# The last feed-forward of a four-layer block: its two-part products in reduced float32 become single products in plain float32

## The reference, cut to what matters

```python
def ternary_quant(w):
    s = jnp.mean(jnp.abs(w))
    q = jnp.clip(jnp.round(w / s), -1.0, 1.0) * s
    return w + jax.lax.stop_gradient(q - w)
w1q = ternary_quant(w1)
w3q = ternary_quant(w3)
w2q = ternary_quant(w2)
h1 = jnp.einsum('bsd,hd->bsh', x, w1q)
h3 = jnp.einsum('bsd,hd->bsh', x, w3q)
g = jax.nn.silu(h1) * h3
return jnp.einsum('bsh,dh->bsd', g, w2q)
...
x = x + jnp.tanh(g_ffn[3]) * _L3_ffn_ref(_layernorm(x, axis=-1), L3_ffn_w1, L3_ffn_w3, L3_ffn_w2)
```

## Time and profile before

| | us |
|---|---|
| median of 3 executions | 2648.24 |
| fastest, slowest | 2644.77, 2649.71 |
| the profiled execution, its own time | 2647.07 |
| its span, first to last instruction | 2645.3 |
| mean granted TensorE clock | 0.947 |
| TensorE matmul busy | 2398.7 (91%) |
| TensorE weight loads busy | 1413.4 (53%) |
| VectorE, ScalarE, GpSimd busy | 992.7, 656.1, 463.8 |

### The profile page before, as it was taken

The page is one execution under the profiler, slowest core; times in us unless marked ns, Lnnn a source line. Parts: engine busy times, 40 slices in busy tenths (PEclk is TensorE's granted clock), DMA queues, the critical chain, the costliest instruction groups (busy, mean ns, idle before and its releaser), DMA issues. The chain is left out here.

```text
span 2645.3 us, 34842 instructions
## 1 busy us (share of the span) xinstructions
PE 2398.7 (91%) x10421; PEld 1413.4 (53%) x10422; DVE 992.7 (38%) x2413; ACT 656.1 (25%) x1456; POOL 463.8 (18%) x616
## 2 busy tenths in 40 slices
PE   7898999988888899998989999695999999789898
PEld 4344444453664566666546654253656665345476
DVE  5534353534334333334412224651222221612375
ACT  2344443530110433433101110110111111051221
POOL 6000000003122100000321114234111111700061
PEclk9999999988999899999889999777999999989999
DMA  9101010013774000000436664150544452561220
GB/s 371 68 1 33 0 33 0 0 33 112 254 227 126 28 17 5 13 13 23 139 102 203 197 194 118 48 160 25 162 131 152 157 170 71 155 211 43 83 84 28
DMA packets 151926, 263.88 MB, mean 100 GB/s; under 512 B 16406, under 2 KB 80510, under 8 KB 151325
## 3 DMA queue, kind: packets, MB, share of 16 engines
q1 hardware_dynamic: 117789, 186.08, 21.8%
q0 software_dynamic: 19072, 49.35, 6.5%
q10 hardware_dynamic: 14976, 27.27, 2.7%
HBM read 212.77 MB, written 49.88 MB: 99 GB/s over the span
## 5 line engine op out<-in xcount | busy, mean ns | idle before, releaser
L360 POOL DMA_INDIRECT slot_list<-token_ids,slots x64 | 62.0, 969 | 620.2 <-DVEq L546 601.3
L924 PE MATMUL bank<-f2r_wd,f2b_hT 128*128 (+1 forms) x300 | 137.2, 593 | 1.4 <-DVE f2b_hT L1028 1.4
L250 PE MATMUL bank<-ident,xn 112*128 112x112 f32 x256 | 59.3, 399 | 86.5 <-DVE xn L226 86.5
L905 PE MATMUL bank<-f2r_wg,f2b_xT 128*128 x400 | 128.9, 466 | 1.6 <-ACT f2b_xT L961 1.3
L905 PE MATMUL bank<-f2r_wu,f2b_xT 128*128 x400 | 126.5, 459 | 0.0
L1355 PE MATMUL bank<-l0a_vo,l0a_zT 128*112 128x512 f32 x256 | 115.5, 594 | 2.9 <-DVE l0a_zT L1513 2.9
L1325 PE MATMUL bank<-l_kvcT,xnT 128*112 128x375 f32 x256 | 98.4, 508 | 20.7 <-DVE l0a_qrT L1485 20.7
L1416 ACT ACTIVATE l0a_p<-l0a_p,l0a_low 112x375 f32<-112x375 f32 x128 | 77.1, 607 | 115.2 <-DVE l0a_low L1506 114.0
L1015 DVE TENSOR_TENSOR f2b_h<-bank,f2b_acted 128x352 f32<-128x352 f32 x50 | 26.2, 525 | 205.9 <-PE bank L905 205.9
L360 POOL DMA_INDIRECT slot_list<-token_ids,slots_in x32 | 31.2, 974 | 408.5 <-DVEq L546 399.3
L1496 DVE CUSTOM_DVE_ANT_0 l0a_p<-bank,xn 112x375 f32<-112x375 f32 x128 | 70.3, 549 | 83.5 <-PE bank L1327 83.3
(11 more groups left out here) (374 smaller groups left out, 4470.0 us busy)
## 6 DMA issues: line engine op xcount, KB each, us to landing
slot_rows<-zeros SPq DMA_DIRECT2D x2, 7424.0 KB
slot_rows<-f2b_y ACTq DMA_DIRECT2D x50, 256.0 KB, 3.7
f1r_wg<-in_l_wg SPq DMA_DIRECT2D x16, 704.0 KB, 4.6
f1r_wu<-in_l_wu SPq DMA_DIRECT2D x16, 704.0 KB, 6.4
f2r_wg<-in_l_wg SPq DMA_DIRECT2D x16, 704.0 KB, 4.4
f2r_wu<-in_l_wu SPq DMA_DIRECT2D x16, 704.0 KB, 6.2
xn<-in_l_w_ffn SPq DMA_DIRECT2D x11, 768.0 KB, 4.2
l_raw<-in_l_w_ffn SPq DMA_DIRECT2D x11, 768.0 KB, 4.2
```

The lines of the kernel that those rows point to most:

```text
L250: mm = pe.transpose(s.bank[n % 4][:, k * TOK:(k + 1) * TOK], s.xn[:, n, k * 128:(k + 1) * 128], s.ident[0:TOK, 0:TOK])
L360: pool.indirect_dma_start(s.slot_list, bass.IndirectOffsetOnAxis(ap=slots[:, k, b:b + 1], axis=0), s.token_ids[:, b:b + 1], None, **bound) ...
L905: mm = pe.matmul(bank[:, 0:width], xT[:, v, k, :], w[:, bass.ds(at, 1), k, :].rearrange("p o f -> p (o f)"), start=(k == 0), stop=(k == KD ...
L924: mm = pe.matmul(bank_y[v][:, :], hT[0:fn, v, c, :], wd[0:fn, bass.ds(at, 1), c, :].rearrange("p o f -> p (o f)"), start=(c == 0), stop=(c ...
```

## The change

The ternary tiles, and the hidden values, become plain float32 tiles, the activations are no longer split, and the parts, their remainders, the tile `h` and the semaphores between them go. `piece(n)` makes 8 calls where it made 16, each on `s.xnT` itself, `output(u)` half as many as well. `hidden(n)` writes straight into `hT` (now one part), and so takes over the wait of L2286 for the output of unit u - 2; output waits for `h_done`. The order of pieces, outputs, ternary tiles and additions stays, and so do the loads.

```diff
--- before.py
+++ after.py
@@ -2197,15 +2197,12 @@
         def sb(n, shape, dt=F32):
             return ctx.enter_context(nc.sbuf_tensor(f"f3_{n}", shape, dt))
 
-        below_done, tern_done, xhi_done, xlo_done, g_done, u_done, act_done, h_done, hi_done, lo_done, y_done, y_added = s.sems(
-            "f3", "below_done", "tern_done", "xhi_done", "xlo_done", "g_done", "u_done", "act_done", "h_done", "hi_done",
-            "lo_done", "y_done", "y_added")
+        below_done, tern_done, g_done, u_done, act_done, h_done, y_done, y_added = s.sems(
+            "f3", "below_done", "tern_done", "g_done", "u_done", "act_done", "h_done", "y_done", "y_added")
         below = sb("below", [128, 2, D])
-        tern = sb("tern", [128, TERNS, 3, D], F32R)
-        xr = sb("xr", [128, 2, KD, NT], F32R)
+        tern = sb("tern", [128, TERNS, 3, D])
         acted = sb("acted", [128, 2, HALF])
-        h = sb("h", [128, 2, HALF])
-        hT = sb("hT", [128, 2, 2, UNIT, NT], F32R)
+        hT = sb("hT", [128, 2, UNIT, NT])
         block = ctx.enter_context(nc.Block())
 
         def halves(half):
@@ -2237,29 +2234,22 @@
                 if n >= 2:
                     pe.wait_ge(h_done, n - 1)
                 for m, done in ((0, g_done), (1, u_done)):
-                    for part in range(2):
-                        if n < 2 and m == 0:
-                            pe.wait_ge((xhi_done, xlo_done)[part], half + 1)
-                        for k in range(KD):
-                            mm = pe.matmul(s.bank[2 * (n % 2) + m][:, 0:HALF],
-                                           tern[:, c % TERNS, m, k * 128:(k + 1) * 128],
-                                           xr[:, part, k, halves(half)],
-                                           start=(part == 0 and k == 0), stop=(part == 1 and k == KD - 1))
+                    for k in range(KD):
+                        mm = pe.matmul(s.bank[2 * (n % 2) + m][:, 0:HALF],
+                                       tern[:, c % TERNS, m, k * 128:(k + 1) * 128],
+                                       s.xnT[:, k, halves(half)], start=(k == 0), stop=(k == KD - 1))
                     mm.then_inc(done, 1)
 
             def output(u):
                 chunks = [c for c in range(L3_CHUNKS) if unit_of[c] == u]
                 pe.wait_ge(tern_done, 3 * chunks[-1] + 3)
-                pe.wait_ge(lo_done, 2 * chunks[-1] + 2)
+                pe.wait_ge(h_done, 2 * chunks[-1] + 2)
                 for b in range(B):
                     if u * B + b >= 4:
                         pe.wait_ge(y_added, u * B + b - 3)
                     for c in chunks:
-                        for part in range(2):
-                            mm = pe.matmul(s.bank[4 + b % 4][0:TOK, :],
-                                           hT[:, u % 2, part, c % UNIT, b * TOK:(b + 1) * TOK],
-                                           tern[:, c % TERNS, 2, :],
-                                           start=(c == chunks[0] and part == 0), stop=(c == chunks[-1] and part == 1))
+                        mm = pe.matmul(s.bank[4 + b % 4][0:TOK, :], hT[:, u % 2, c % UNIT, b * TOK:(b + 1) * TOK],
+                                       tern[:, c % TERNS, 2, :], start=(c == chunks[0]), stop=(c == chunks[-1]))
                     mm.then_inc(y_done, 1)
 
             for n in range(PIECES):
@@ -2270,23 +2260,12 @@
 
         @block.scalar
         def _(act):
-            for half in range(2):
-                act.activation(xr[:, 0, :, halves(half)], s.xnT[:, :, halves(half)], ACT.Copy).then_inc(xhi_done, 1)
-            for n in range(PIECES + 1):
-                if n < PIECES:
-                    act.wait_ge(g_done, n + 1)
-                    if n >= 2:
-                        act.wait_ge(h_done, n - 1)
-                    act.activation(acted[:, n % 2, :], s.bank[2 * (n % 2)][:, 0:HALF], ACT.Silu,
-                                   scale=t.scale[:, 0:1]).then_inc(act_done, 1)
-                if n >= 1:
-                    c, half = (n - 1) // 2, (n - 1) % 2
-                    u = unit_of[c]
-                    act.wait_ge(h_done, n)
-                    if u >= 2:
-                        act.wait_ge(y_done, (u - 1) * B)
-                    act.activation(hT[:, u % 2, 0, c % UNIT, halves(half)], h[:, (n - 1) % 2, :], ACT.Copy)\
-                       .then_inc(hi_done, 1)
+            for n in range(PIECES):
+                act.wait_ge(g_done, n + 1)
+                if n >= 2:
+                    act.wait_ge(h_done, n - 1)
+                act.activation(acted[:, n % 2, :], s.bank[2 * (n % 2)][:, 0:HALF], ACT.Silu,
+                               scale=t.scale[:, 0:1]).then_inc(act_done, 1)
 
         @block.vector
         def _(dve):
@@ -2300,27 +2279,16 @@
                                              scalar=t.half[:, m:m + 1], in1=below[:, i % 2, :],
                                              op0=ALU.is_gt, op1=ALU.subtract).then_inc(tern_done, 1)
 
-            def rest_of_xnT(half):
-                dve.wait_ge(xhi_done, half + 1)
-                dve.tensor_tensor(xr[:, 1, :, halves(half)], s.xnT[:, :, halves(half)],
-                                  xr[:, 0, :, halves(half)].bitcast(F32), ALU.subtract).then_inc(xlo_done, 1)
-
             def hidden(n):
+                c, half = n // 2, n % 2
+                u = unit_of[c]
                 dve.wait_ge(u_done, n + 1)
                 dve.wait_ge(act_done, n + 1)
-                if n >= 2:
-                    dve.wait_ge(hi_done, n - 1)
-                    dve.wait_ge(lo_done, n - 1)
-                dve.scalar_tensor_tensor(out=h[:, n % 2, :], in0=s.bank[2 * (n % 2) + 1][:, 0:HALF],
+                if u >= 2:
+                    dve.wait_ge(y_done, (u - 1) * B)
+                dve.scalar_tensor_tensor(out=hT[:, u % 2, c % UNIT, halves(half)], in0=s.bank[2 * (n % 2) + 1][:, 0:HALF],
                                          scalar=t.scale[:, 1:2], in1=acted[:, n % 2, :],
                                          op0=ALU.mult, op1=ALU.mult).then_inc(h_done, 1)
-
-            def rest_of_hidden(n):
-                c, half = n // 2, n % 2
-                u = unit_of[c]
-                dve.wait_ge(hi_done, n + 1)
-                dve.tensor_tensor(hT[:, u % 2, 1, c % UNIT, halves(half)], h[:, n % 2, :],
-                                  hT[:, u % 2, 0, c % UNIT, halves(half)].bitcast(F32), ALU.subtract).then_inc(lo_done, 1)
 
             def add(u):
                 for b in range(B):
@@ -2331,19 +2299,13 @@
                                              scalar=t.output_scale[0:TOK, :], in1=s.x[:, b, :],
                                              op0=ALU.mult, op1=ALU.add).then_inc(y_added, 1)
 
-            make_ternary(0, (0, 1))
-            rest_of_xnT(0)
-            rest_of_xnT(1)
-            make_ternary(0, (2,))
+            make_ternary(0, range(3))
             for n in range(PIECES):
                 if n % 2 == 0 and n // 2 + 1 < L3_CHUNKS:
                     make_ternary(n // 2 + 1, range(3))
                 hidden(n)
-                if n:
-                    rest_of_hidden(n - 1)
                 if n > 1 and n % (2 * UNIT) == 1:
                     add(unit_of[n // 2] - 1)
-            rest_of_hidden(PIECES - 1)
             add(units - 1)
```

## The result

| | before | after |
|---|---|---|
| median, us | 2647.41 (4 runs) | 2740.77 (4 runs) |
| fastest, slowest | 2644.77, 2649.71 | 2738.04, 2742.50 |
| profiled execution, its own time | 2647.07 | 2739.71 |
| its span | 2645.3 | 2738.0 |
| TensorE in the stage, first gate/up record to the end of the last output record | 119.8 | 211.5 |

The changed kernel takes 1.0353 times as long, with a 95% interval of 1.0337 to 1.0369: 93 us more. The kernel before has one execution more here than it had at the time of the prediction, 2646.59 us, which moves its median from 2648.24 to 2647.41.

What follows compares the result with a forecast made beforehand. TensorE was taken as the bound: gate/up 132.4, output 75.5, start 2.2, last seam 0.8 and modelled ends 0.3 make 211.2 us against 119.8. That adds 91.4 to 2648.24, giving 2739.6 us, range 2735 to 2744.5.

Steps and rivals of the forecast that it cites:

- The price of a record: TensorE's last feed-forward: 352 gate/up records at 0.376 us make 132.4 us, 176 output records at 0.429 make 75.5.
- The start: First gate/up pieces: TensorE starts at 2516.46 again, and 4.5 us at half clock lose 2.2 us.
- modelled end: Last records before the last seam and of the stream: shown ends lie past the start distance, 0.3 us together.
- The last seam: Before the last output: TensorE waits for `hidden` alone, 0.8 us in place of 2.09.
- The stretch: TensorE's whole stream in the last feed-forward: 211.2 us against 119.8.
- Cover: Last feed-forward: nothing on VectorE or GpSimd is waited for after 2520; TensorE alone is late.
- Splitting: Remainders on VectorE, 16.3 us for the hidden values, cost only the first pieces' wait and the seams.
- same records at the same price: Rival for TensorE's stream: record count matters, not type; 115.9 us, 3.9 less, 2644.3; chance 0.01.
- The rule on weight loads: TensorE's full-height loads: hidden beside the matmul by the trace, against the skill page; the sum counts none.
- The rival of loads in the open: Each TensorE weight load stands between matmuls: 305.4 us in place of 207.9, time 2837; chance 0.005.
- One record per call: Rival: float32 calls leave one record at today's price, TensorE needs 56.3 us, GpSimd sets the end, 2590.8; chance 0.01.

Runs made afterwards that it cites:

- The run with the clock kept up: Changed kernel with six more float32 matmuls of 448 columns ahead of the first piece; stretch 209.0 us, 1.0315 times the kernel before.
- the run on the fourth chip: The changed kernel itself, measured again on another chip against the kernel before there; stretch 211.1 us, ratio 1.0342.
- the doubled kernel: Changed kernel with float32r operands, each call made twice on the same rounded part, remainders left out; stretch 115.1 us, 0.9987 times the kernel before.
- the kernel cut to 224 columns: Kernel before with each gate/up call cut into two of 224 moving columns; stretch 124.8 us, one run of 2693.5 us beside a median of 2692.2.
- The one-part kernel: Changed kernel with float32r operands, one call each on the rounded part, remainders left out; stretch 77.6 us, 0.9836 times the kernel before.

## Why the prediction was right, point by point

The median is 2740.77 for a forecast of 2739.6; the profiled execution took 2739.71 for 2738.5, its span 2738.0 for 2736.7. The rise is 93.4 us by the medians and 92.6 by the profiled executions, for 91.4.

- **The price of a record.** 36.08 / 96 = 0.376 and 20.60 / 48 = 0.429 us, as read from L2026, L2033 and L741. The counts stayed. These two terms are 207.9 of the 211.5 us.
- **The start.** TensorE waited for the same two tiles. The clock rose 4.7 us after the first record where I took 4.5; the first 128 records cost 50.71 - 128 x 0.376 = 2.6 us too much, of which 0.16 are the modelled end that the sum counts apart, so 2.4 where the sum has 2.2. The run with the clock kept up shows that this is the clock's. That it came so close is in part luck: in the run on the fourth chip the clock rose 4.0 us after the first record, and in the one with float32 in gate/up only 5.1, behind the same idle stretch.
- **The last seam.** 0.82 us for 0.8.
- **The stretch.** 211.5 for 211.2.
- **The rest of the 1.3 us of span.** The stage's loads begin 0.7 us later (2500.40 for 2499.71), ahead of anything changed, and the first record 0.2 later behind that.
- **Cover.** No wait for `f_below` or `f_tern` reached TensorE after the first. The waits of VectorE for TensorE grew instead: the additions waited 52.8 us.
- **Splitting.** It was put at nothing but stall and seams; the doubled kernel gives it 4.7 us of stretch. The forecast's own way of counting it (same records at the same price) gave 3.9; most of the rest is the 0.234 us of an output record, read too high by the modelled end that it holds (0.230 in a stream without seams).
- **The rule on weight loads.** The Trainium skill, page "TensorE: Matmul & The Clock Gate", section "The mechanism" (the prediction named the section behind it), lets a load overlap matmuls in flight only in another row group. The trace disagrees more plainly than the prediction had it: a full-height load takes 112 ns of a stream of 8 columns, and with 224 columns, 93 ns at 2.4 GHz, the records still stand 112 ns apart (the kernel cut to 224 columns). One after the other they would take 205.
- **What was right for too weak a reason.** I argued that today's loads of 192 ns fit a distance of 203 ns. That reads as though loads were nearly the bound of a float32r call. They are not, since a load takes 112 ns of the stream; my expectation for the 224 columns rested on it and missed by some 60 us. The rival of loads in the open was priced by the shown durations, 190 and 174 ns (the second is the median of L2259's loads in the trace and stands in no row shown); at 112 ns for each of the 528 it would have come at most 59 us later than the forecast, not 97.5.
- **A rival that was too low.** "One record per call" was put at 2590.8 by GpSimd's busy time. The one-part kernel shows such a stage: 42 us less than before, not 57, since VectorE's row of tiles, hidden values and additions is the longer one and TensorE's clock fell in the waits.

## What to carry to other kernels

Count the records that a call leaves before counting calls: a plain float32 product leaves two, each two cycles per column, so it costs 3.7 float32r products, and two float32r products on a split operand are the cheaper way as long as the split hides elsewhere. Two are enough here because the weights are -1, 0 and 1 and need no second part; a product of two general operands would need more, and no run here prices that. Splitting that looks like much work (16 us on VectorE) was worth under 5 us here, since TensorE was the bound; the idle engines' busy time is no saving. The same shapes elsewhere in a kernel, read from start to start in a stretch at full clock, give a new type's price to half a per cent. The duration that a trace shows for a weight load says little of its cost; a stream with few moving columns does.

## What the runs showed of the hardware that was not expected

- At a granted clock of 1.00 a float32r call costs its columns at 2.4 GHz plus 16 ns (0.203 us for 448 columns, 0.230 for 512), a bfloat16 call plus 2.5 (0.189 for 448, 0.216 for 512), a float32 record twice its columns plus 2.5 (0.376, 0.429).
- A weight load of 128 x 128 in float32 or float32r, shown with 192 to 195 ns, takes 0.112 us of the stream at 1.00 and 0.213 at 0.50, and costs nothing where the columns beside it take longer. What a bfloat16 load, shown with 100 ns, takes was not measured.
- The chips differ: the kernel before takes 2647 us on one and 2689 to 2692 on three others, while TensorE's stretch in this stage in the changed kernel is the same to 0.4 us (211.5 and 211.1). The cause is open.
